# Graph attention on Trainium2: main loops written out, with one register load per step

## The reference

```python
Qh = (h @ WQ).reshape(N, H, D)
Kh = (h @ WK).reshape(N, H, D)
Vh = (h @ WV).reshape(N, H, D)
Eh = (edge_attr @ WE).reshape(-1, H, D)
score = jnp.einsum('ehd,ehd,ehd->eh', Kh[src], Qh[dst], Eh) * inv_sqrt_d
score = jnp.exp(jnp.clip(score, -5.0, 5.0))
msg = Vh[src] * score[:, :, None]
wV = jax.ops.segment_sum(msg, dst, num_segments=N)
Z = jax.ops.segment_sum(score, dst, num_segments=N)
h_out = wV / (Z[:, :, None] + 1e-06)
out = _layernorm(x + h_out.reshape(N, H * D), axis=-1)
```

## Time and profile before

| | |
|---|---|
| median of 3 runs | 3138.6 us |
| span of the profiled execution | 3220.4 us |
| its own time beside the span | not given |
| mean granted clock of PE | 0.758 |
| busy, PE matmul / weight load | 66% / 60% |
| busy, DVE / ACT / POOL | 48% / 41% / 48% |
| DMA, mean over the span | 106 GB/s |
| instructions recorded | 56767 |

### The profile page before, as it was taken

One profiled execution on the slowest core, in us unless ns is written; L12 is line 12 of the kernel. 1 busy time (PEld: TensorE's weight loads), 2 busy tenths in 40 slices (PEclk: granted clock), 3 DMA queues, 4 the chain that ended last, 5 costly groups with the idle time before them and its releaser, 6 DMA issues.

```text
span 3220.4 us, 56767 instructions
## 1 busy us (share of the span) xinstructions
PE 2141.5 (66%) x14786; PEld 1940.1 (60%) x14787; DVE 1538.8 (48%) x3801; ACT 1316.4 (41%) x3270; POOL 1547.9 (48%) x1628
## 2 busy tenths in 40 slices
PE   6566666666766666666766666666666666666666
PEld 5466656665655666665666556656556665666565
DVE  4444444454444544444444444444444444544446
ACT  2344443444434444344444344443444444444343
POOL 3444444454544445444545444544444554445542
PEclk8677777777777777777777777777777778777777
DMA  7533333333333333333333333333333333333331
GB/s 214 150 102 100 105 102 103 103 101 101 107 102 102 102 103 105 102 101 103 101 106 103 103 102 99 104 104 102 103 102 100 106 105 101 102 104 105 104 105 56
DMA packets 222816, 339.98 MB, mean 106 GB/s; under 512 B 92112, under 2 KB 117688, under 8 KB 222795
## 3 DMA queue, kind: packets, MB, share of 16 engines
q0 software_dynamic: 77376, 211.39, 22.2%
q1 hardware_dynamic: 144843, 128.08, 14.7%
q10 hardware_dynamic: 576, 0.26, 0.0%
HBM read 325.24 MB, written 9.60 MB: 104 GB/s over the span
## 4 chain that ended last, share of the span: by engine, by line
another core or an unknown queue 32%; PE 22%; issue 21%; DVE 15%; DVEq 7%; ACT 2%; ACTq 1%; DMA 0%; SPq 0%
PE psW L578 12%; PE psE L544 4%; DVE msg L919 4%; DVEq L244 4%; PE psT L535 3%; DVE acc L936 3%; PE psH L554 2%; DVE prod L897 2%; DVE prod L902 2%; DVE score L907 1%; DVEq L936 1%; DVEq L948 1%; ACT hot L709 1%; DVEq L894 1%
## 5 line engine op out<-in xcount | busy, mean ns | idle before, releaser
L434 POOL DMA_INDIRECT kv<-kv_table,src_idx x1612 | 1539.4, 955 | 1620.1 <-DVE msg L919 1118.6
L578 PE MATMUL psW<-msg,hot 128*128 128x136 f32 x3224 | 665.3, 367 | 462.3 <-DVE msg L919 461.5
L722 ACT ACTIVATE attrT<-psT 128x512 f32<-128x512 f32 x403 | 240.8, 597 | 1665.2 <-remote 1213.7
L578 PEld LDWEIGHTS psW<-msg,hot 128*128 128x128 f32 x3224 | 567.3, 257 | 522.3 <-DVE msg L919 380.4
L544 PE MATMUL psE<-w_e,attrT 128*128 128x128 f32 x3224 | 592.2, 320 | 177.6 <-issue 175.6
L902 DVE TENSOR_TENSOR prod<-prod,psQ 128x512 f32<-128x512 f32 x403 | 276.8, 687 | 855.4 <-remote 848.5
L567 PE MATMUL psQ<-Qp,hotT 128*128 x4836 | 458.3, 242 | 265.4 <-issue 263.9
L544 PEld LDWEIGHTS psE<-w_e,attrT 128*128 128x128 f32 x3224 | 517.8, 234 | 193.0 <-issue 191.7
L567 PEld LDWEIGHTS psQ<-Qp,hotT 128*128 128x128 bf16 x4836 | 365.3, 110 | 371.0 <-issue 364.2
L709 ACT ACTIVATE hot<-iota,local 128x128 f32 x1612 | 512.0, 390 | 4.4 <-issue 2.5
L897 DVE TENSOR_TENSOR prod<-kv,psE 128x512 f32<-128x512 f32 x403 | 277.2, 688 | 339.9 <-issue 170.8
(11 more groups left out here) (94 smaller groups left out, 362.5 us busy)
## 6 DMA issues: line engine op xcount, KB each, us to landing
attr<-in_edge_attr_dram SPq DMA_DIRECT2D x403, 256.0 KB
kv<-kv_table,src_idx POOLq DMA_INDIRECT x1612
src_idx<-in_src_dram SPq DMA_DIRECT2D x403, 2.0 KB
kv_table<-kv SPq DMA_DIRECT2D x12, 512.0 KB, 3.8
Qp<-Qp SPq DMA_DIRECT2D x23, 192.0 KB
hot<-in_x_dram SPq DMA_DIRECT2D x12, 256.0 KB, 4.4
xT<-in_x_dram SPq DMA_DIRECT2D x8, 384.0 KB
out_dram<-xT SPq DMA_DIRECT2D x46, 64.0 KB
```

The lines of the kernel that those rows point to most:

```text
L434: nc.gpsimd.indirect_dma_start(out=kv[:, u, t, :], out_offset=None, in_=kv_table, in_offset=bass.IndirectOffsetOnAxis(ap=src_idx[:, u, t:t ...
L578: last = nc.tensor.matmul(psW[:, u % 2, 0:MW], hot[:, u % HOTS, t, :], msg[:, u % 2, t, :], start=(t == 0), stop=(t == TILES - 1))
```

## The change

The hardware loops of the main work become plain Python loops, so that their bodies stand 49 times in the program (on SP 48 times) with constants in all waits and addresses that came from `b`. The load of eight values at the head of each body becomes a load of one value at the head of each step, on PE, ACT and DVE. Number and order of the engines' and of the DMA instructions stay as they were, and so do all buffers. In short:

```diff
 @@ SP
-            with sp.Fori(2, LAG + 2) as b:
+            for b in range(2, LAG + 2):
                 load_turn(b)
-            with sp.Fori(LAG + 2, B_LAST) as b:
+            for b in range(LAG + 2, B_LAST):
                 load_turn(b)
                 store_window(b - (LAG + 2))
 @@ POOL
-            with pool.Fori(1, B_LAST) as b:
+            for b in range(1, B_LAST):
                 for u in range(RINGS):
                     gather(b, u)
 @@ PE
-            with pe.Fori(1, B_LAST) as b:
-                slots = load_slots(b * RINGS + 1, RINGS)
+            for b in range(1, B_LAST):
                 for u in range(RINGS):
-                    step(b, u, slots[u])
+                    step(b, u, load_slots(b * RINGS + u + 1, 1)[0])
 @@ ACT
-            with act.Fori(1, B_LAST) as b:
-                odd = load_odd(b * RINGS + 3, RINGS)
+            for b in range(1, B_LAST):
                 for u in range(RINGS):
-                    step(b, u, odd[u])
+                    step(b, u, load_odd(b * RINGS + u + 3, 1)[0])
 @@ DVE
-            with dve.Fori(1, LAG) as b:
-                windows = load_windows(b * RINGS - 1, RINGS)
+            for b in range(1, LAG):
                 for u in range(RINGS):
-                    step(b, u, windows[u])
+                    step(b, u, load_windows(b * RINGS + u - 1, 1)[0])
             dve.wait_ge(x_res_in, 16 * (RINGS + 1))
-            with dve.Fori(LAG, B_LAST) as b:
-                windows = load_windows(b * RINGS - 1, RINGS)
+            for b in range(LAG, B_LAST):
                 for u in range(RINGS):
-                    step(b, u, windows[u], b - LAG)
+                    step(b, u, load_windows(b * RINGS + u - 1, 1)[0], b - LAG)
```

## The result

The kernel after takes **3052.5 us** (median of 4 runs, 3048.97 to 3062.27) against 3139.9 us before (4 runs, 3130.92 to 3145.64): ratio **0.9726**, 95% interval 0.9702 to 0.975. That is 87 us, where 13 were forecast, and outside the range.

What follows compares the result with a forecast made beforehand. No engine near full: a two-group cycle bound by gathers, a halt ending some 1.5 us after the last gather, and DVE's chain. 3138.6 us with terms -13.2 + 0 + 0 + 0 gave 3125.4 us; range 3110 to 3180.

Steps and rivals of the forecast that it cites:

- Waits on constants: Register arithmetic ahead of waits goes on five engines; claimed 0 us, at most 40 us gained if it was not covered.
- the stop: Engines other than POOL halt during POOL's second set of gathers, until some 1.5 us after the last gather; reason not seen.
- The fast rival of this cause: Register arithmetic ahead of waits was exposed, so removing it gains 40 us more: 3085 us, chance 0.03.
- The frame under it: Cycle of two groups: short interval, gathers, all engines halted until some 1.5 us after the last gather, then DVE's chain.
- The turn's end and the loads: On PE, ACT and DVE: removing eight-value loads and branch gains 13.2 us; one load per step stays hidden, 0 us.
- The rival of the loads: On DVE behind line 897, single loads delay line 902's wait: +40 us, 3178 us, chance 0.14.
- Code fetch: Straight code brings about 145 packets on q8 and 108 on q14; claimed 0 us, at most 77 us.
- The reading of the span: Profiled span 3220.4 us against median 3138.6 us: the 81.8 us, 2.6%, were put down to the profiler.
- the alternation of a short and a long interval: Between DVE's messages, 5.42 us and 10.34 us take turns in the main loops; expected to be kept.
- jumps refill nothing: Going back to a loop body's head fetches no code; the opposite rival claimed 49 us gained, 3090 us, chance 0.04.

Runs made afterwards that it cites:

- e1: Against the kernel before: all loops written out with constant waits, eight values loaded at each turn's head; 3030.4 us, ratio 0.9666.
- e2: Against the kernel before: all five loops kept, but one value loaded at each step on PE, ACT and DVE; 3196.7 us, ratio 1.0181.
- e14: Against the kernel before, on a chip without stops: everything written out, eight values loaded at each turn's head; 2147.6 us against 2138.8, ratio 1.0044.
- e6: Against the kernel before, on a chip without stops: POOL's loop alone written out; ratio 1.0003.

## Why the prediction was wrong, step by step

**The step that failed** is "Waits on constants": "0 us; if the cover were gone, under 0.1 us per group, 40 us gained at most". On a chip with stops, constants in place of registers, with the branches of the loops, bring 109 us (e1). I had the register work down as run ahead of queued work, in the engines' idle time. But much of the idle time is the stop, and in the stop a register operation can take 0.71 us. The trace of before said so: the assertions of ACT with up to 727 ns stand in the very view from which I took the loads' 595 ns, and I read only DVE's and PE's medians. The fast rival of this cause got 0.03 and 40 us, and these 40 us came from the supposed stretch by the profiler, not from anything in the kernel. That the register work is what holds DVE in the stop is argued from these runs; that it has to go for the gain, and brings none without stops, is shown.

**The frame under it** was that the stop ends "some 1.5 us after the last gather", whatever the engines have to do. DVE's end of it is not fixed: its median went from 1.55 us after the last gather to the last gather's end, and in e1 to 1.44 us ahead of it, while ACT's stayed 1.4 to 1.7 us after it.

**The turn's end and the loads.** Forecast: 13 us gained by removing eight values per turn, nothing lost by one per step. The runs with and without this part, all else equal, are after and e1: 3052.5 against 3030.4, 22 us lost. With loops it is 58 us lost (e2). The traces show both sides. The long interval at a turn's end is 10.49 us in the mean in before, where the three others of a turn have 10.05: 0.44 us exposed per turn and not the 0.27 that I read from one. In e1 it is 9.69 against 8.74, in after 9.09 against 9.35. So the turn's end was indeed removed, and more than paid for in the other long intervals. The size of a single load was right (0.30 us), and in the pair above it doesn't hold DVE up, whose line 895 starts 0.73 us after its message:

```profile
1513.32 0.69 DVE L895 TENSOR_TENSOR prod<-kv,psE 128x512 f32<-128x512 f32 x1
```

That the operations of three engines count in sum, of which after has more than e1 (51048 instructions against 50019), is likely and was not shown. The rival of the loads had the right sign for this part and, by this pair, the wrong place. The Trainium skill says in "DMA: Bandwidth & Descriptors", section "Latency and other measured facts", that the compiler unrolls by four to spread a load's cost. That one load for eight values is cheaper than eight loads (e1, e2) agrees with it; the floor of about 600 ns that it gives doesn't agree with the 301 ns measured here for one value.

**Code fetch.** About 145 and 108 packets were forecast; the whole trace has 133 and 134. With stops their cost can't be told from the rest. Without, written-out code costs 0.44% (e14), 9 us, of which POOL's gathers have 7; that the fetches do this was not shown.

**The reading of the span.** I explained the 2.6% between span and median by the profiler. A run of the kernel after took 3055.2 us with a span of 3053.4: it stretches next to nothing. The gap was a sign that executions of one kernel differ by chip.

**What was right:** the alternation of a short and a long interval (5.42 us kept, the long one 9.08), that the long one has the gathers and the stop in it, that jumps refill nothing, that the turn's end can be removed, and the size of a load and of the code traffic.

**Still open:** why the engines stop while POOL gathers, why some chips don't, what the steps of 0.71 us are, why DVE is the one let go earlier, how the gain divides between branches and register arithmetic, and DVE's own share of it on a chip with stops.

## What to carry to other kernels

An idle time put down to "remote" is to be explained before anything beside it is priced at zero: look in it for sequencer operations that take many times their usual length, on every engine. Where they are there, register operations, branches and moves can cost, even on an engine that is far ahead. Here writing the loops out with constants was then worth 3.3%, and one load for eight values was better than eight loads. Measure such a change on several chips: the same one was 2.7% faster on one and 0.6% slower on another, and the best version without a cap on gathers (e1, 0.9666 with stops) loses 0.4% without stops. The capped one, 0.9315 with stops, loses 10.7%.

## What the runs showed of the hardware that was not expected

- The same program took 2139 us on three chips, 3139 us on a fourth and 3218 us on a fifth, and the runs on each lay within 0.5% of one another.
- On the slow ones ACT, DVE and SP stand still while POOL issues its second set of gathers, and PE goes on in steps of some 0.7 us. DVE was let go 1.4 us ahead of the last gather's end, at it, or 1.4 to 1.6 us after it, by kernel, and ACT 1.4 to 1.7 us after it in all. POOL itself keeps its 0.95 us per gather.
- There, 369 operations of the sequencers of SP, ACT, DVE and PE took 0.6 to 0.8 us each, where the medians of register operations, moves and assertions in the same trace are 18 to 123 ns by engine and kind. The branch of SP's loop has a median of 701 ns there and of 45 ns in e6, without stops.
